# Geometric attention blocks ahead of the standard ones, and values and sums as two pieces

## The reference

```
xn  = layernorm(x)
q,k,v = xn Wq (8 heads of 32), xn Wk, xn Wv (2 heads each, shared by 4 query heads); rotary on q, k
std = softmax(causal(q k^T / sqrt(32))) v
geo = softmax(causal(qp kp)) v      # qp, kp: one number per head and token (3 channels dot a fixed direction)
att = (std + head_scales * (geo - std)) Wo
z   = xn ternary(W_syn)^T + b_syn;  hidden = relu(z) where z is among the top 102 of its 1024, else 0
ffn = layernorm(xn + hidden ternary(W_out)^T + b_out) * gamma + beta
out = x + att + ffn
```

## Time and profile before

| | |
|---|---|
| median of 3 runs | 785.08 us (782.65 to 787.91) |
| profiled execution | 785.15 us, span 783.4 us |
| PE busy | 703.4 us (90%), mean granted clock 0.896 |
| DVE, ACT, POOL busy | 495.6 (63%), 464.9 (59%), 262.5 (34%) |

### The profile page before, as it was taken

One profiled execution on the slowest core, in us unless ns is written; L12 is line 12 of the kernel. 1 busy time (PEld: TensorE's weight loads), 2 busy tenths in 40 slices (PEclk: granted clock), 3 DMA queues, 4 the chain that ended last, 5 costly groups with the idle time before them and its releaser, 6 DMA issues. The chain is left out here.

```text
span 783.4 us, 12828 instructions
## 1 busy us (share of the span) xinstructions
PE 703.4 (90%) x4536; PEld 351.5 (45%) x4536; DVE 495.6 (63%) x1022; ACT 464.9 (59%) x789; POOL 262.5 (34%) x390
## 2 busy tenths in 40 slices
PE   2779889989999997999999997799999999989954
PEld 1445434455344344543344334544544455554434
DVE  3798498854675686266474648274575576856463
ACT  3354762058654611765554461688889888988930
POOL 5516562043214104331030102302433543343355
PEclk9876987589799975999999898899999999999986
DMA  8100000000000000000000000000000000000000
GB/s 234 63 1 4 7 2 7 0 3 1 1 8 1 1 1 2 1 5 6 1 1 1 1 2 1 10 1 8 8 8 8 8 8 15 8 8 8 2 0 28
DMA packets 12373, 9.41 MB, mean 12 GB/s; under 512 B 5713, under 2 KB 11729, under 8 KB 12306
## 3 DMA queue, kind: packets, MB, share of 16 engines
q1 hardware_dynamic: 12306, 8.55, 3.8%
HBM read 5.80 MB, written 2.10 MB: 10 GB/s over the span
## 5 line engine op out<-in xcount | busy, mean ns | idle before, releaser
L728 ACT ACTIVATE probs<-scores 128x1024 f32<-128x1024 f32 (+3 forms) x320 | 269.8, 893 | 153.9 <-PE acc L1208 56.3
L1208 PE MATMUL acc<-probs,v_nat 128*32 128x512 f32 (+3 forms) x1280 | 159.0, 570 | 6.1 <-POOL probs L606 5.8
L1208 PE MATMUL acc<-probs,ones_all 128*32 128x512 f32 (+3 forms) x1280 | 153.7, 553 | 0.0
L926 DVE TENSOR_REDUCE piece_max<-side 128x1 f32<-128x512 f32 x156 | 103.5, 686 | 73.9 <-PE side L1107 72.9
L606 POOL TENSOR_SCALAR_AFFINE_SELECT probs<-probs 128x256 f32<-128x256 f32 x128 | 57.9, 463 | 156.8 <-ACT probs L728 155.8
L1107 PE MATMUL side<-k_stack,q_stack 96*128 96x512 f32 (+3 forms) x232 | 93.5, 462 | 3.7 <-DVE piece_max L926 1.8
L1188 PE MATMUL scores<-q_stack,k_stack 98*128 98x512 f32 (+3 forms) x320 | 92.2, 398 | 2.4 <-ACT probs L728 2.4
L1208 PEld LDWEIGHTS acc<-probs,ones_all 128*32 128x32 f32 x1280 | 43.0, 115 | 82.9 <-issue 80.1
L1107 PEld LDWEIGHTS side<-k_stack,q_stack 96*128 96x128 f32 x232 | 42.1, 203 | 71.2 <-issue 45.6
L1188 PEld LDWEIGHTS scores<-q_stack,k_stack 98*128 98x128 f32 x320 | 55.3, 195 | 27.5 <-ACT probs L728 19.1
L641 POOL TENSOR_TENSOR xb<-xn,b_down 128x256 f32<-128x256 f32 x16 | 12.4, 776 | 147.8 <-DVE y_mv L1059 138.3
(11 more groups left out here) (144 smaller groups left out, 1105.9 us busy)
## 6 DMA issues: line engine op xcount, KB each, us to landing
res<-in_L_attn_x_dram SPq DMA_DIRECT2D x4, 512.0 KB, 9.2
out_dram<-res SPq DMA_DIRECT2D x16, 128.0 KB, 1.7
z_buf<-in_L_ffn_W_syn_dram SPq DMA_DIRECT2D x1, 1024.0 KB, 7.8
z_buf<-in_L_ffn_W_out_dram SPq DMA_DIRECT2D x1, 1024.0 KB, 4.9
k_geo<-geo_rows SPq DMA_DIRECT2D x24, 8.0 KB
q_geo<-geo_rows SPq DMA_DIRECT2D x24, 8.0 KB
w_qkv<-in_L_attn_Wq_dram SPq DMA_DIRECT2D x1, 256.0 KB, 4.4
tables<-in_cos_table_dram SPq DMA_DIRECT2D x1, 256.0 KB, 4.5
```

Source lines behind the costliest of these rows:

```text
L728: nc.scalar.activation(probs[:, slot % 2, pair, :, off:], scores[:, pair, :, off:], ACT.Exp, scale=ATT_SCALE if kind == 0 else 1.0).then_i ...
L926: free(nc.vector.tensor_reduce(piece_max[:, h, p:p + 1], pt, AX.X, ALU.max), ("S",) + a)
L1208: last = nc.tensor.matmul(acc[D * h:D * h + D, part, off:], lhs, probs[:, slot % 2, h // 2, h % 2, off:], start=first, stop=end)
```

## The change

In every chunk both geometric blocks come first, group 0 and 1, then both standard blocks. So the first of a group to be stored in `mixed` is the geometric one, and the four-step mix now runs on the standard block's output with the parts turned round. q_geo keeps one buffer: its DMAs for chunk c wait for the last sum of the geometric blocks of chunk c-1. The operation vs is cut into "val" (four matmuls with the values, rank 13) and "sum" (four with ones, rank 12.5); they stand in the same flow, and all that waited for vs waits for sum.

```diff
+KINDS = ((1, 0), (1, 0), (1, 0), (1, 0))
...
-            wait = [("vs", c - 2, G - 1, 1, TPC * (c - 1) - 1)] if c >= 2 else []
+            wait = [("sum", c - 2, G - 1, 0, TPC * (c - 1) - 1)] if c >= 2 else []
...
         add("geo", "sp", 1, ("geo_dma", c), 8000, [("geo_top", c), ("geo_lo", c), ("geo_hi", c), ("fill",)]
-            + ([("vs", c - 2, G - 1, 1, TPC * (c - 1) - 1)] if c >= 2 else []))
+            + ([("sum", c - 1, G - 1, 1, TPC * c - 1)] if c >= 1 else []))
...
-    slots = [(c, g, kind, j) for c in range(NCH) for g in range(G) for kind in range(2) for j in range(TPC * (c + 1))]
-    epilogues = [(c, g, kind) for c in range(NCH) for g in range(G) for kind in range(2)]
+    slots = [(c, g, kind, j) for c in range(NCH) for kind in KINDS[c] for g in range(G) for j in range(TPC * (c + 1))]
+    epilogues = [(c, g, kind) for c in range(NCH) for kind in KINDS[c] for g in range(G)]
...
-                + ([("vs",) + slots[n - 2]] if n >= 2 else []))
+                + ([("sum",) + slots[n - 2]] if n >= 2 else []))
...
-        add("vs", "pe", 13, ("vs", c, g, kind, j), 60 + 1700 * share,
+        add("val", "pe", 13, ("val", c, g, kind, j), 30 + 870 * share,
             [("cut" if j >= TPC * c else "exp", c, g, kind, j, PAIRS - 1)]
             + ([("o_raw",) + epilogues[e - 1], ("d_raw",) + epilogues[e - 1]] if j == 0 and e else []), "columns")
+        add("val", "pe", 12.5, ("sum", c, g, kind, j), 30 + 870 * share, [("val", c, g, kind, j)], "columns")
...
-        add("mix", "pool", 2, ("mix", c, g, kind), 1350 if kind == 0 else 5700,
-            [("recip", c, g, kind), ("late",)] + ([("unit", "o", TPC * c - 1)] if kind == 0 and c else []))
+        add("mix", "pool", 2, ("mix", c, g, kind), 1350 if kind == KINDS[c][0] else 5700,
+            [("recip", c, g, kind), ("late",)] + ([("unit", "o", TPC * c - 1)] if kind == KINDS[c][0] and c else []))
...
-        q_geo = sb("q_geo", [P, 2, G, CHUNK], F32R)
+        q_geo = sb("q_geo", [P, G, CHUNK], F32R)
...
-                    if c >= 2:
-
-                        sp.wait_ge(probs_used, acc_done[2 * G * (c - 1) - 1])
+                    if c >= 1:
+
+                        sp.wait_ge(probs_used, acc_done[epi_no[(c - 1, G - 1, 1)]])
...
-                        link(nc.gpsimd.tensor_tensor(o_raw[:], o_raw[:], mixed[:, g], ALU.subtract))
-                        link(nc.gpsimd.tensor_scalar(o_raw[:], o_raw[:], scale_h[:, g:g + 1], None, ALU.mult))
-                        link(nc.gpsimd.tensor_tensor(mixed[:, g], o_raw[:], mixed[:, g], ALU.add))
+                        std, geo = (o_raw[:], mixed[:, g]) if kind == 0 else (mixed[:, g], o_raw[:])
+                        link(nc.gpsimd.tensor_tensor(geo, geo, std, ALU.subtract))
+                        link(nc.gpsimd.tensor_scalar(geo, geo, scale_h[:, g:g + 1], None, ALU.mult))
+                        link(nc.gpsimd.tensor_tensor(mixed[:, g], geo, std, ALU.add))
...
-                    for part, lhs in enumerate((v_nat[:, j, g], ones[:, 0:D])):
-                        for h in range(HG):
-                            last = nc.tensor.matmul(acc[D * h:D * h + D, part, off:], lhs,
-                                                    probs[:, slot % 2, h // 2, h % 2, off:], start=first, stop=end)
+                    for h in range(HG):
+                        nc.tensor.matmul(acc[D * h:D * h + D, 0, off:], v_nat[:, j, g],
+                                         probs[:, slot_no[a] % 2, h // 2, h % 2, off:], start=(j == 0), stop=(j == TPC * (c + 1) - 1))
+                if k == "sum":
+
+                    c, g, kind, j = a
+                    off = max(0, j - TPC * c) * P
+                    for h in range(HG):
+                        last = nc.tensor.matmul(acc[D * h:D * h + D, 1, off:], ones[:, 0:D],
+                                                probs[:, slot_no[a] % 2, h // 2, h % 2, off:], start=(j == 0), stop=(j == TPC * (c + 1) - 1))
                     last.then_inc(probs_used, 1)
```

More of the change, by code:

```diff
@@ L157, in build_plan @@
         e = epilogues.index((c, g, kind))
-        add("vs", "pe", 13, ("vs", c, g, kind, j), 60 + 1700 * share,
+        add("val", "pe", 13, ("val", c, g, kind, j), 30 + 870 * share,
             [("cut" if j >= TPC * c else "exp", c, g, kind, j, PAIRS - 1)]
             + ([("o_raw",) + epilogues[e - 1], ("d_raw",) + epilogues[e - 1]] if j == 0 and e else []), "columns")
+        add("val", "pe", 12.5, ("sum", c, g, kind, j), 30 + 870 * share, [("val", c, g, kind, j)], "columns")
     for e, (c, g, kind) in enumerate(epilogues):
-        last = [("vs", c, g, kind, TPC * (c + 1) - 1)] + [("mix",) + epilogues[e - 1]] * (e > 0)
+        last = [("sum", c, g, kind, TPC * (c + 1) - 1)] + [("mix",) + epilogues[e - 1]] * (e > 0)
         add("epi", "act", 0, ("d_raw", c, g, kind), 600, last)
@@ L165, in build_plan @@
         add("recip", "dve", 2, ("recip", c, g, kind), 3400, [("d_raw", c, g, kind), ("o_raw", c, g, kind)])
-        add("mix", "pool", 2, ("mix", c, g, kind), 1350 if kind == 0 else 5700,
-            [("recip", c, g, kind), ("late",)] + ([("unit", "o", TPC * c - 1)] if kind == 0 and c else []))
+        add("mix", "pool", 2, ("mix", c, g, kind), 1350 if kind == KINDS[c][0] else 5700,
+            [("recip", c, g, kind), ("late",)] + ([("unit", "o", TPC * c - 1)] if kind == KINDS[c][0] and c else []))
     for t in range(NT):
-        unit("o", 0, ("o", t), 860, [("mix", t // TPC, G - 1, 1)])
+        unit("o", 0, ("o", t), 860, [("mix", t // TPC, G - 1, KINDS[t // TPC][1])])
         add("o", "dve", 0, ("o_add", t), 430, [("unit", "o", t)], empties=("o", t))
@@ L278, in attention_and_ternary_ffn @@
     score_no = {key[1:]: n for key, n in number("pe", "score").items()}
-    slot_no = {key[1:]: n for key, n in number("pe", "vs").items()}
+    slot_no = {key[1:]: n for key, n in number("pe", "sum").items()}
     cut_no = {key[1:]: n for key, n in number("pool", "cut").items()}
@@ L515, in _ @@
                             at = GROWS * g + r
-                            sp.dma_start(q_geo[at:at + 97:32, b, g, :].bitcast(F32), src.bitcast(F32)).then_inc(geo_in[c], 16)
+                            sp.dma_start(q_geo[at:at + 97:32, g, :].bitcast(F32), src.bitcast(F32)).then_inc(geo_in[c], 16)
                 if k == "w_next":
@@ L617, in _ @@
                                 "p (g h) -> p g h", g=G)[:, :, h]))
-                    if kind == 0:
+                    if kind == KINDS[c][0]:
                         if c >= 1:
@@ L694, in _ @@
                     if c >= 2:
-                        act.wait_ge(probs_used, acc_done[2 * G * (c - 1) - 1])
+                        act.wait_ge(probs_used, acc_done[epi_no[(c - 2, G - 1, 0)]])
                     free(nc.scalar.copy(q_stack[0:STK, c % 2, 4 * half:4 * half + 4, col:col + P],
@@ L1192, in _ @@
                             last = nc.tensor.matmul(dst[:, off:], k_geo[rows, P * j:P * j + P],
-                                                    q_geo[rows, b, g, off:], start=True, stop=True)
+                                                    q_geo[rows, g, off:], start=True, stop=True)
                     last.then_inc(score_full, 1)
-                if k == "vs":
+                if k == "val":
                     c, g, kind, j = a
-                    slot, e = slot_no[a], epi_no[a[:3]]
+                    e = epi_no[a[:3]]
                     off = max(0, j - TPC * c) * P
-                    first, end = j == 0, j == TPC * (c + 1) - 1
                     if j >= TPC * c:
@@ L1203, in _ @@
                         pe.wait_ge(probs_ready, score_no[a + (PAIRS - 1,)] + 1)
[L1204 removed]
+                    if j == 0 and e >= 1:
                         pe.wait_ge(raw_ready, 2 * e)
[L1206 to L1209 removed]
+                    for h in range(HG):
[7 more added lines that the diff above has]
+                                                probs[:, slot_no[a] % 2, h // 2, h % 2, off:], start=(j == 0), stop=(j == TPC * (c + 1) - 1))
                     last.then_inc(probs_used, 1)
```

3 lines of the change are left out of this document (1 added, 2 removed).

## The result

The changed kernel takes **774.39 us** (median of 4 runs, 771.86 to 776.71) against 785.05 us for the kernel before beside it (782.65 to 787.91): ratio 0.985, 95% interval 0.982 to 0.988. Its profiled execution took 772.55 us, span 770.6. That is inside the stated range (738 to 802) and inside the forecast's own (755 to 777), 6 us above the forecast of 768, but the experiments show that the terms of its sum are not what they were taken for.

What follows compares the result with a forecast made beforehand. The prediction took the kernel as TensorE bound, with three holes, a slow start and a tail. From 785.15 us it took 31 for fill, added 26 for breaks and took 12 for feed: 768, range 738 to 802.

Steps and rivals of the forecast that it cites:

- Step 1: Geometric blocks first fill the three stretches without exponentials, less chunk 0's later start: 31 us gained, bounds 13 and 40.
- Rival C: Effects cancel: holes fill, but moved work returns nothing later; breaks 26, no feed gain: 784 us, chance 0.21.
- Step 2: Cut pair feeds VectorE and ScalarE at half the grain in the long stretches: 12 us gained, bounds 0 and 20.
- Step 3: Work put between val and sum makes TensorE change shape: 128 breaks, 34 us, 26 on the path, bounds 8 and 50.
- The rule of the Trainium skill: Any tiling change drains the array; row-tiled breaks would then cost as much as others, 40 us in place of 34.
- last attention block: Sign of right: attention's end near 743 us instead of 760, with the tail as long as before, 23 us.
- exponentials in the old holes: Sign of right: exponentials of scores from q_geo run in the former holes, no stretch over 15 us without after 90.
- room outside start and tail: Sign that the whole is wrong: TensorE's unused full-clock time between start and tail stays near 95 us.
- breaks in 7 of 10 slots: Sign of right: val blocks followed by scores or a unit in 8 of 10 slots.
- a granted clock near 1: Sign of right: TensorE's granted clock near 1 in what were the holes.
- S of chunk 1: Sign that part 1, the block order, is wrong: this S stage ends past 165 us.
- ScalarE's wait behind matmul blocks: Sign that part 2, the cut, is wrong: ScalarE's idle time behind matmul blocks grows past 56 us.

Runs made afterwards that it cites:

- e1: Changed kernel with values and sums as one piece again, leaving only the new block order: 840.62 us, ratio 1.071 to the kernel before.
- e5: Changed kernel's plan, but on TensorE every sum stands directly behind its val, all other queues unchanged: 789.42 us.
- e2: Kernel before with only the pair cut into val and sum; block order, q_geo buffers and mix as before: 792.11 us.
- e6: Changed kernel with val and sum cut only in chunks 0 to 2; in chunk 3 the sum follows its val: 773.15 us.
- e9: Changed kernel with SLACK 100 and, in chunk 3, sum rank 11.5, so units but not scores may go ahead of it: 755.08 us.

## Why the prediction was right, and where not

**The range was right, the sum by luck.** Room less work: the prediction had 43 us off (31 fill, 12 feed) and 26 on; measured were 34.4 off and 21.4 on. Each is somewhat smaller and the net is 13 instead of 17. But the prediction's two parts, taken one by one, were to give 754 (order) and 799 (cut), and gave 840.6 and 792.1: the total came out near because an error of 87 us in one part was made up by an interaction that the sum doesn't have.

**Step 1, the fill (31, "S pieces now have two banks instead of six ... I take 85%").** This is the step that failed as a step. The holes did fill, with exponentials from q_geo, as told. But the harm to S (fewer banks, fewer turns) was priced at 15% of the fill, some 5 us, and with whole pieces it is far more: order alone is 55 us slower than before (48 at SLACK 130), where the step would have given 785 - 31 = 754. What was late next was S itself. The rows to see it were there: VectorE is busy 81% and 89% of the first two holes and 62% and 55% of the long stretches behind them, so a hole of ScalarE was also the time in which S was served best. Banks and turns weren't separated; the 30 pieces in banks of the scores in the changed kernel, against 37 in e1, speak for turns. Rival C named this mechanism ("S of the next chunk, through two banks, ends as late as before and the feed-forward tiles behind it too") but priced it at 4 us.

**Step 2, the feed gain (12).** Right in kind, and put on the wrong account. In the changed kernel the cut is worth 66 us (840.6 to 774.4), because S is served more often per slot: 15 us of it by the places between val and sum, 51 by the rest of the list that the planner then writes (e5). The prediction let it act "only on the room in the three long stretches" and on the 56.3 us of waits; that bound was wrong. The cut also closes two of the holes by bringing S forward (e2), so steps 1 and 2 claimed in part the same room. On the old order the cut is worth nothing net (+7, -1).

**Step 3, the breaks (128, 34 us gross, 26 on the path).** Counted in the lists, 117 of 160 slots are broken, 105 with full-array work in them. TensorE leaves the column shape 247 times instead of 155, because many units only moved from between slots to within one. The price per break was right for a break by full-array work. Timeline of TensorE at full clock, standard slots: unbroken, then broken by a pair of scores (start, length).

```profile
711.36 1.04 PE L1209 MATMUL acc<-probs,v_nat 128*32 128x512 f32 x8
712.21 1.04 PE L1216 MATMUL acc<-probs,ones_all 128*32 128x512 f32 x8
...
715.69 1.06 PE L1209 MATMUL acc<-probs,v_nat 128*32 128x512 f32 x8
716.69 0.73 PE L1191 MATMUL scores<-q_stack,k_stack 98*128 98x512 f32 x2
717.35 1.07 PE L1216 MATMUL acc<-probs,ones_all 128*32 128x512 f32 x8
```

From val to what follows it is 0.85 us unbroken and 1.00 broken; a pair of scores between two column blocks takes 0.66, and in e6 four of them in one go 1.14 (707.09 to 708.23), half of which is 0.57. A break so costs 0.15 for leaving, and 2 x 0.66 - 1.14 = 0.18 for the second return: 0.33, against 0.31 predicted. 92 more departures at 0.31 are 29 us; the work rose by 21, or by 25 in windows of 10 us. Closing the breaks in place (e5, 656 us of work) took back only 7 of those 25, while the kernels without a cut lie at 633 to 648 and those cut in every chunk at 660 to 668. What makes up the rest in e5 stays open, so the 21 us aren't shown to be breaks alone. A part may be row-tiled scores that are issued in two pairs (last section).

The rule of the Trainium skill, "TensorEngine Tiling (Array Packing)", Key Properties, that a change of tiling mode drains the array, was read in the prediction as making row-tiled breaks as dear as the others. A geometric slot broken by all four of its scores:

```profile
555.97 1.06 PE L1209 MATMUL acc<-probs,v_nat 128*32 128x512 f32 x8
556.97 0.51 PE L1195 MATMUL scores<-q_geo,k_geo 10*128 10x512 f32 x4
557.41 1.06 PE L1216 MATMUL acc<-probs,ones_all 128*32 128x512 f32 x8
```

Leaving is 1.00 against 0.88 (557.41 to the next val at 558.29), and the four scores take 0.44, as outside a break (729.08 to 729.52 before): 0.12 in all, not 0.33. So a drain may happen at each change, but its price is not the same for each. One reading was off: the slot of 2.29 us in the earlier trace rows has only two of the four scores in it (724.59, x2; two others stand at 722.30, ahead of its first val). The time stands, because four together take no longer than two, but a slot whose two pairs come apart costs more (last section), and the prediction had no term for that.

**The tail and the ends.** Predicted: last attention block near 743, tail 23 us. Measured: 751.0 and 19.6. Not foreseen: the feed-forward part, which ended last before (776.2), ends at 733.8, and what closes the kernel is now attention with its mix.

**The signs set beforehand.** As told: exponentials in the old holes, none missing for more than 8.4 us, first scores at 86.42, room outside start and tail 62 instead of 96. Nearly: breaks in 7 of 10 slots, where 8 were forecast. Only in part: a granted clock near 1 (0.82, 1.00 and 0.87 in the three old holes). Two signs said "wrong" and one of them rightly. S of chunk 1 ended at 173, past 165 (156 before): the first hole gave next to nothing, for the room from 61 to 190 us is 32.9 against 36.3 before (windows of 10 us). ScalarE's wait behind matmul blocks rose from 56.3 to 188.3, far past the 56 that was to condemn the cut; but e6 has 163.1 and e9 172.6 and they are as fast or faster. That sign was a bad one. The likely reason, not tested: ScalarE has to wait somewhere, since TensorE bounds it, and the releaser only tells what it waited for last.

## What to carry to other kernels

Filling a hole of one engine takes the turns of whoever used the hole: ask which chain was served there (here S through two banks and VectorE), and what then ends last. Two halves of a change can each lose and together gain, so before splitting a sum into additive terms, check whether two terms claim the same room. A run that undoes one half in the finished order (e5) tells what the half does on the chip from what it does to the planner. And where a planner writes the order, a tie-break constant can move the time as much as the change; repeat the comparison at a second value before believing its size.

## What was not expected of the hardware

Two row-tiled scores cost as much time as four (timeline of the changed kernel):

```profile
507.92 0.50 PE L1195 MATMUL scores<-q_geo,k_geo 10*128 10x512 f32 x2
508.35 1.06 PE L1209 MATMUL acc<-probs,v_nat 128*32 128x512 f32 x8
...
510.72 0.51 PE L1195 MATMUL scores<-q_geo,k_geo 10*128 10x512 f32 x4
511.16 1.07 PE L1216 MATMUL acc<-probs,ones_all 128*32 128x512 f32 x8
```

The two take 0.43 us and the four 0.44. A geometric slot whose two pairs of heads are issued apart therefore pays 0.42 us more (2 x 0.43 - 0.44), which is more than the 0.33 of a break; the group's busy time rose from 51.0 us before to 58.0 after. The full-array scores don't behave so (0.66 for two, 1.14 for four). Keeping both pairs of a geometric slot together wasn't tried.
